# A new timetable for the last stage of a four-layer kernel: gating by half, four gate buffers, and a chain of small steps divided between VectorE and GpSimd

## The reference, cut to what matters

```python
def _L1_ffn_ref(x, Wm, bm, expert_emb, W1, b1, W2, b2, Wo, bo):
    BS, L, D = (4, 256, 128);  H, E, K = (8, 16, 2);  HD = D // H;  I = 512 // H
    h = x @ Wm + bm
    t = h.reshape(bs * L_ * H, HD)
    w = softmax(t @ expert_emb)                       # 16 weights for each head
    topw, topi = top_k(w, K)                          # ties: the lower index
    hmid = gelu(einsum('td,edi->tei', t, W1) + b1)    # 16 experts, 64 hidden each
    eo = einsum('tei,eio->teo', hmid, W2) + b2
    comb = (take_along_axis(eo, topi) * topw).sum(axis=1)
    return comb.reshape(bs, L_, d) @ Wo + bo
# x = x + _L1_ffn_ref(_layernorm(x), ...)
```

## Time and profile before

| | us |
|---|---|
| median of 3 runs | 2245.03 (2243.67 to 2245.81) |
| the profiled execution's own time | 2241.12 |
| its span | 2239.1 |
| head experts, first prologue matmul to the end | about 1770 to 2239 |
| of its stretch 1820 to 2239: PE busy / DVE / ACT / POOL | 399.3 / 300.1 / 284.1 / 86.5 of 419 |

### The profile page before, as it was taken

The page is one execution under the profiler, slowest core; times in us unless marked ns, Lnnn a source line. Parts: engine busy times, 40 slices in busy tenths (PEclk is TensorE's granted clock), DMA queues, the critical chain, the costliest instruction groups (busy, mean ns, idle before and its releaser), DMA issues. The chain is left out here.

```text
span 2239.1 us, 44674 instructions
## 1 busy us (share of the span) xinstructions
PE 1840.9 (82%) x16984; PEld 1141.9 (51%) x16984; DVE 1063.2 (47%) x2449; ACT 1334.1 (60%) x1479; POOL 214.8 (10%) x158
## 2 busy tenths in 40 slices
PE   3447999999994788787888878787887379999998
PEld 2337998989992443343443433343443145555554
DVE  6895222222225334433444334344441577777774
ACT  0013444444440597777778778677888156766675
POOL 7712000000003000000000000000000001211112
PEclk9567999999996799999999999899999589999999
DMA  6201000000002332133332222233220100000000
GB/s 220 52 14 41 1 1 1 1 2 1 1 1 56 69 74 58 41 73 74 71 73 59 68 56 51 64 73 71 58 58 5 56 1 6 6 5 5 5 5 10
DMA packets 37267, 88.90 MB, mean 40 GB/s; under 512 B 11481, under 2 KB 24034, under 8 KB 36466
## 3 DMA queue, kind: packets, MB, share of 16 engines
q1 hardware_dynamic: 33906, 78.82, 14.7%
q0 software_dynamic: 3072, 6.30, 1.4%
HBM read 33.15 MB, written 2.10 MB: 16 GB/s over the span
## 5 line engine op out<-in xcount | busy, mean ns | idle before, releaser
L1157 ACT ACTIVATE C_probs<-C_ps_s 128x1024 f32<-128x1024 f32 x832 | 781.9, 1070 | 243.5 <-PE C_ps_s L1084 241.3
L1097 PE MATMUL C_ps_o<-C_probs,C_values 128*16 128x256 f32 x6656 | 477.5, 401 | 30.1 <-DVE C_o_t L1270 16.1
L1592 ACT ACTIVATE D_hidden<-D_ps_u,D_b_up 128x1024 f32<-128x1024 f32 x256 | 275.3, 1113 | 150.0 <-PE D_ps_u L1508 149.9
L1084 PE MATMUL C_ps_s<-C_queries,C_keys 32*128 32x256 f32 x3328 | 222.2, 343 | 145.9 <-issue 59.5
L692 ACT ACTIVATE B_hidden<-B_ps_h,B_b_up 128x512 f32<-128x512 f32 x288 | 194.1, 687 | 187.8 <-PE B_ps_h L620 185.8
L1084 PEld LDWEIGHTS C_ps_s<-C_queries,C_keys 32*128 32x128 f32 x3328 | 133.8, 194 | 326.3 <-ACT C_probs L1157 174.7
L633 PE MATMUL B_ps_e<-B_w_down,B_hidden 128*128 128x128 f32 x2304 | 274.9, 276 | 0.0
L633 PEld LDWEIGHTS B_ps_e<-B_w_down,B_hidden 128*128 128x128 f32 x2304 | 269.9, 192 | 8.3
L1097 PEld LDWEIGHTS C_ps_o<-C_probs,C_values 128*16 128x16 f32 x6656 | 157.1, 98 | 193.9 <-issue 49.1
L1609 POOL TENSOR_TENSOR D_gated<-D_gated 128x1024 f32<-128x1024 f32 x32 | 76.2, 2382 | 1427.3 <-DVE D_gated L1725 1427.3
L787 DVE SCALAR_TENSOR_TENSOR B_acc<-B_ps_e,B_gate,B_acc 128x128 f32<-128x128 f32 x224 | 63.1, 344 | 289.2 <-PE B_ps_e L633 289.2
(11 more groups left out here) (259 smaller groups left out, 1967.9 us busy)
## 6 DMA issues: line engine op xcount, KB each, us to landing
C_keys<-C_k_hi SPq DMA_DIRECT2D x128, 200.1 KB, 4.3
C_ctx_t<-ctx_t_dram SPq DMA_DIRECT2D x16, 800.5 KB, 4.3
C_keys<-C_k_lo SPq DMA_DIRECT2D x64, 200.1 KB, 4.1
C_queries<-C_q_hi SPq DMA_DIRECT2D x128, 32.0 KB, 1.9
B_w_up<-L_ffn_w_up_dram SPq DMA_DIRECT2D x1, 2304.0 KB
B_w_down<-L_ffn_w_down_dram SPq DMA_DIRECT2D x1, 2304.0 KB, 20.8
A_ids<-ids_dram SPq DMA_DIRECT2D x1, 2048.0 KB
C_queries<-C_q_lo SPq DMA_DIRECT2D x64, 32.0 KB, 1.9
```

The lines of the kernel that those rows point to most:

```text
L1084: m = T.matmul(ps_s[bank(parity, 2 * step + j // 2)][:, j % 2, i, :], keys[rows, parity, g, kt * P:(kt + 1) * P], queries[rows, parity, g, ...
L1097: m = T.matmul(ps_o[32 * j:32 * j + 2 * DK, g % 2, :], values[:, parity, kt, g * HG + j, :], probs[:, slot(parity, 2 * step + j // 2), j % ...
L1157: nc.scalar.activation(probs[:, slot(parity, n)], ps_s[bank(parity, n)][:], ACT.Exp, scale=SCORE_SCALE1).then_inc(s_exp, 1)
L1592: nc.scalar.activation(hidden[:, u % RING, :, :], ps_u[u % 2][:], ACT.Gelu, bias=b_up[:, u % PAIRS:u % PAIRS + 1]).then_inc(s_hid, 1)
```

## The change

The tables are spread out: a job every even unit, a down piece every odd unit, and an out part every even unit from 14 on. Gating is done for each head (128x512) with a ring of four gate buffers. The exponential moves from unit 6 to unit 8, the first preparing job (turn) from 2 to 1, the turn_gate jobs from 26 and 30 to 29 and 31. Of the 16 steps of the choice, five go to GpSimd, and so do the two subtractions that make the low parts; each hand-over is a semaphore (`s_choice`). GpSimd's order within a block is written out in `body`.

```diff
+        PIECES = 2 * QUADS
+        GRING = 4
-        gate = sb("gate", [P, 2, 2, BLOCK])
+        gate = sb("gate", [P, GRING, BLOCK])
-        PREPARE = {2: ("turn", 0), 3: ("project", 0), 6: ("logit", 0), 7: ("place_up", 0), 10: ("place_up", 1),
-                   14: ("place_up", 2), 18: ("place_up", 3), 26: ("turn_gate", 0), 30: ("turn_gate", 1)}
+        PREPARE = {1: ("turn", 0), 3: ("project", 0), 5: ("logit", 0), 7: ("place_up", 0), 11: ("place_up", 1),
+                   15: ("place_up", 2), 25: ("place_up", 3), 29: ("turn_gate", 0), 31: ("turn_gate", 1)}
-        GATES = {4 * v + s: ("place_gate", (v, s)) for v in range(QUADS) for s in range(2)}
+        GATES = {2 * m: ("place_gate", m) for m in range(PIECES)}
-        EXP_AT, SPLIT_AT = 6, 25
+        EXP_AT = 8
-        CHOOSE_AT = {9: (0, 1, 2), 10: (3,), 13: (4,), 14: (5,), 17: (6, 7, 8), 18: (9,), 21: (10, 11, 12),
-                     22: (13,), 23: (14,), 24: (15,)}
+        CHOOSE_AT = {9: (0, 1), 11: (3,), 13: (4,), 17: (6, 7), 19: (8, 9), 21: (10,), 23: (12, 13)}
+        POOL_CHOICES = (2, 5, 11, 14, 15)
-        DOWN_AT = timetable((4 * v + 5 + s, (v, s)) for v in range(QUADS) for s in range(2))
-        GATING_AT = timetable((4 * v + 6, v) for v in range(QUADS))
-        OUT_AT = timetable((8 * hp + 15 + (0, 1, 4, 5)[n], (hp, n)) for hp in range(HP) for n in range(4))
+        DOWN_AT = timetable((2 * m + 5, (m,)) for m in range(PIECES))
+        GATING_AT = timetable((2 * m + 6, m) for m in range(PIECES))
+        OUT_AT = timetable((8 * hp + 14 + 2 * n, (hp, n)) for hp in range(HP) for n in range(4))
         X_AT = 13
         HEADS_AT = 4
+        SPLIT_AT = 27
...
+                def body(k, before, prepares):
+                    if before:
+                        add_groups(k - 1, HP - 1)
+                    if prepares:
+                        lower_heads(k + 1)
+                        choose(k + 1, 2)
+                    if before:
+                        add_bias(k - 1)
                     add_groups(k, 0)
-                    add_bias(k - 1)
-                    for hp in range(1, HP - 1):
-                        add_groups(k, hp)
+                    if prepares:
+                        choose(k + 1, 5)
+                    add_groups(k, 1)
+                    if prepares:
+                        choose(k + 1, 11)
+                        choose(k + 1, 14)
+                        choose(k + 1, 15)
+                    add_groups(k, 2)
+                    if prepares:
+                        lower_gates(k + 1)
...
-                    V.scalar_tensor_tensor(to, ps_e[:], b_down[:, v % EG:v % EG + 1], gate[:, v % 2],
+                    V.scalar_tensor_tensor(to, ps_e[:, s], b_down[:, v % EG:v % EG + 1], gate[:, piece % GRING],
                                            ALU.add, ALU.mult).then_inc(s_read, 1)
```

More of the change, by code:

```diff
@@ L1497, in job @@
                     else:
-                        v, s = arg
+                        v, s = divmod(arg, 2)
                         half, h = divmod(v // EG * 2 + s, HG1)
@@ L1510, in up, with down @@
                     m.then_inc(s_up, 1)
[L1512 to L1515, removed]
+                def down(k, piece):
+                    v, s = divmod(piece, 2)
+                    pe.wait_ge(s_hid, UNITS * k + 4 * v + 4)
+                    wait(pe, s_read, PIECES * k + piece - 1)
                     for i in range(4):
@@ L1566, in _ @@
                 pe.wait_ge(s_job_done, jobs_before(BLOCKS - 1) + NGATE)
-                for s in range(2):
-                    down(BLOCKS - 1, QUADS - 1, s)
+                for what, of_before in DOWN_AT.values():
+                    if of_before:
+                        down(BLOCKS - 1, *what)
                 for hp, n in (what for what, of_before in OUT_AT.values() if of_before):
@@ new lines, in choose @@
+                def choose(p, step):
+                    pool.wait_ge(s_choice, CHOICE_STEPS * p + step)
+                    if step == 2:
+                        ins = G.tensor_tensor(weight[:], weight[:], total[:].unsqueeze(2).to_broadcast(CHOICES),
+                                              ALU.mult)
+                    elif step == 14:
+                        ins = G.tensor_tensor(chosen[:, 0], chosen[:, 0], chosen[:, 1], ALU.add)
+                    elif step == 15:
+                        ins = G.tensor_tensor(weight[:], weight[:], chosen[:, 0], ALU.mult)
+                    else:
+                        ins = G.tensor_tensor(hit[:], hit[:], order[:].unsqueeze(1).to_broadcast(CHOICES), ALU.mult)
+                    ins.then_inc(s_choice, 1)
@@ L1654, in job @@
                     else:
-                        v, s = arg
-                        wait(dve, s_read, QUADS * p + v - 1)
-                        done = V.tensor_copy(gate[:, v % 2, s, :], ps_p[:])
+                        wait(dve, s_read, PIECES * p + arg - GRING + 1)
+                        done = V.tensor_copy(gate[:, arg % GRING, :], ps_p[:])
                     done.then_inc(s_job_done, 1)
@@ L1737, in experts @@
                     for u in range(UNITS):
+                        if u in GATING_AT:
+                            piece, of_before = GATING_AT[u]
+                            if not of_before:
+                                gating(k, piece)
+                            elif not first:
+                                gating(k - 1, piece)
                         if u in at:
@@ L1771, in _ @@
                         for step in range(CHOICE_STEPS):
-                            choose(0, step)
+                            if step not in POOL_CHOICES:
+                                choose(0, step)
                         split_gates(0, 0)
@@ L1784, in _ @@
                 rounds(dve, BLOCKS, experts)
-                gating(BLOCKS - 1, 1, QUADS - 1)
+                for piece, of_before in GATING_AT.values():
+                    if of_before:
+                        gating(BLOCKS - 1, piece)
                 add_to_stream(BLOCKS - 1)
```

78 lines of the change are left out of this document (38 added, 40 removed).

## The result

| | median, us | runs | against before |
|---|---|---|---|
| before | 2244.35 | 2242.51 to 2245.81 | |
| changed | 2332.16 | 2330.66 to 2334.06 | 1.0392 (95%: 1.0374 to 1.0410) |

What follows compares the result with a forecast made beforehand. TensorE's own pace was taken to bound the kernel. Steady blocks of 49.9 us work plus 12.3 waits, +8.6 six times, with first and last blocks, prologue and end summed to +61.7: median 2306 us, range 2278 to 2325.

Steps and rivals of the forecast that it cites:

- The quad: TensorE's four ups, two gates, two outs and two downs without preparing jobs: 5.64 us in the even timetable, 5.76 before.
- The jobs: A preparing block's nine extra TensorE jobs, priced by similar matmuls: 4.8 us per block.
- the gain of 3.7 a block: Per preparing block: 2.7 us of waiting won back and 1.0 us from the even timetable's shorter quads.
- unit 14, bias ahead of add: First head pair's out part waits for GpSimd's add behind add_bias: 3.5 us a block, 2.6 in the last.
- unit 29, low part behind add: turn_gate waits for the gates' low part, behind the third pair's add on GpSimd: 2.95 us a block.
- exponential: Up in unit 11 waits for ScalarE's chain with the exponential and two table loads: 2.3 us a block.
- turn: Turn job in unit 1 waits for VectorE's normalizations behind the copy of gate 0: 1.15 us a block.
- units 6, 7, 25: VectorE late after the cast of h and step 10 wait out GpSimd adds: 2.4 us of TensorE waiting per block.
- prologue: Without cover, five choice steps and the gates' low part on GpSimd lengthen the prologue: +4.1 us.
- Rival 1: Even timetable wins, all hand-overs hidden, first pair's add ending within 3.6 us of up 12's start: 2222 us; chance 0.06.
- Rival 2: Only GpSimd's order bites: waits in units 14 and 29 stay, others absorbed, gains come: 2266 us; chance 0.13.
- Rival 3: GpSimd is slower in the chain, including about 1 us for its loop turn, +2.4 per block: 2323 us; chance 0.13.

Runs made afterwards that it cites:

- filled_waits: Changed kernel with 12 spare TensorE matmuls ahead of each of two long waits (turn_gate in unit 29, first out part in unit 14); 1.0313 against before.
- both_orders: Changed kernel with, on GpSimd, the first pair's add ahead of the bias and the gates' low part ahead of the third pair's add; 1.0173 against before.
- the mended kernel: Changed kernel, GpSimd's orders mended, normalizations first in unit 0, exponential behind gelu 6, h rounded in unit 3, two steps moved, VectorE's loop written out; 1.0011.
- before_shared: Kernel before with only choice steps 2, 5, 11, 14 and 15 moved to GpSimd, old timetable and whole gatings; 1.0027 against before.
- before_bias_ahead: Kernel before with one edit: GpSimd's add_bias stands ahead of the first pair's add; 1.0087 against before.

## Why the prediction was wrong in its size

The mechanism of the waits was right, step by step, and the sum too small by 26 us (24 in the stage of the two traces). The step that failed is the sentence "TensorE's own work in a preparing block is 8 x 5.64 + 4.8 = 49.9 us", taken at full clock throughout. It failed twice.

*The clock.* I had seen 1.00 in the earlier trace rows and carried it into a kernel whose waits I had myself put at 3.5 and 2.95 us. Behind those TensorE ran at half clock. In the blocks 1 to 5 of the changed kernel (1877.65 to 2209.23) it is busy 277.8 us, 17.3 more than five times 52.1, with twelve stretches at half clock in them. That is 1.4 us for each, and by this price about 23 us for all sixteen, which is an estimate. filled_waits, which takes twelve of the sixteen away, gives back 1.0392 - 1.0313 = 0.0079, or 18 us.

*The pace.* At full clock a block's own work is 52.1 (both_orders), not 49.9. The quad was right: 5.60 against 5.64. The jobs weren't: priced at 4.8 by their kin, they cost 52.1 - 44.8 = 7.3. Between an up and a down, where a plain odd unit takes 1.64, the units with a job take 2.73 (project) and 2.76 (logit), so these cost 1.09 and 1.12 instead of 0.77 and 0.9. They are the smaller part of the miss. By the same distances in block 1 of both_orders, waits left out, the four place_up cost 0.72, 0.48, 0.74 and 0.73 (2.67, where 1.8 was booked), turn and the two turn_gates 0.65, 0.53 and 0.53 (1.7 for 1.3), and three times an even unit takes 1.40 to 1.43 instead of 1.16 where TensorE starts again behind a wait (0.75, booked nowhere). Timeline of PE of the changed kernel, starts:

```profile
1945.54 0.72 PE L1515 MATMUL D_ps_u<-D_up_in,D_w_up_r 128*128 128x512 f32 x2
1946.21 1.13 PE L1490 MATMUL D_ps_p<-D_xt,D_wm 128*128 128x512 f32 x2
1947.27 1.06 PE L1524 MATMUL D_ps_e<-D_hidden,D_w_down 128*32 128x512 f32 x8
1948.27 0.73 PE L1515 MATMUL D_ps_u<-D_up_in,D_w_up_r 128*128 128x512 f32 x2
```

The same error sat in the kernel before: "53.6 - 46.1 - 4.8 = 2.7 us of waiting" was 1.2 of waiting and 52.4 of work. So the gain of 3.7 a block (2.7 and 1.0) that I credited to the even timetable was never there: its own work is 0.3 us a block less (52.1 against 52.4), and what it could win back was 1.2, or 2.4 behind a loop turn. In the mended kernel it won none of it.

*The waits* were forecast at 12.3 a block. Measured are 10.0 between a short turn wait and the next, and 11.8 where the long one falls in:

| term | forecast | measured |
|---|---|---|
| unit 14, bias ahead of add | 3.5 (last block 2.6) | 2.95 (2.23) |
| unit 29, low part behind add | 2.95 | 2.82 |
| exponential | 2.3 | 2.18 (block 0: 2.99) |
| turn | 1.15 | 0.99, every second one 2.78 |
| units 6, 7, 25 | 2.4 | 0.55 (unit 6) + 0.55 (unit 25) |
| half gating | 0.72 | 0.745 |
| prologue | +4.1 | +3.5 |

Unit 14 came out shorter because add_to_stream ran 2.2 behind up 12 (1964.91) where I had 2.6. In units 6, 7 and 25 the lock came as forecast, with 1.93 for the cast and 2.29 for step 10, but less of it reached TensorE than I had booked. Two readings were wrong without weight in the sum: a hand-over to GpSimd takes 0.2 and not 0.05 to 0.1 (in the earlier trace rows add_to_stream ends at 1934.77 and the bias starts at 1934.98), and up didn't lose 0.4 to the exponential in the steady blocks before, where its rows show no idle time. The low work and the high waits nearly cancel: with its waits filled, a block takes 62.1 where 62.2 was forecast. What is left is the clock, by far the most of it, and the loop turn, which makes the turn's wait 1.8 us longer twice. Taking it out gives 1.0392 - 1.0339 = 0.0053 or 12 us by the ratios, whose intervals leave some 5 us either way, and 7.6 us in the stage of the two traces. For the loop turn I had the rows and took only one of them: the earlier trace rows are 53.58, and the next pair of turns was 54.82 apart; I took the quicker for all. In the old timetable, whose turn stood a unit later, only 1.2 to 1.4 of it reached TensorE.

*The rivals.* Rival 1 is refuted on both counts, its condition (the add in time) and its prize. Rival 2 named the two waits rightly, and mending both gives back 49 us; they were not alone. Rival 3 gives 2323, the nearest number of all, by a mechanism that isn't there: GpSimd's add takes 2.36, its bias 1.27, and no wait of TensorE shows a loop turn of GpSimd. That would have been luck.

Left open: why the same wait, of 2.8 us or of 2.2, is followed by half clock in one block and not in another; why VectorE's loop turn costs nothing in before_shared; and where the 2.8 us per block of before_bias_ahead go.

## What to carry to other kernels

Where a forecast contains a wait of a saturated TensorE near 3 us, book the half clock behind it too, here about 1.4 us for each, and count waits near 2 us as a risk of it; filling the wait with spare matmuls tests it in one run. Price a moved job by the distance between the starts on both sides of its place, in a unit that has it and one that hasn't, and not by the duration of its kin; and check a figure for "waiting" obtained by subtraction against the idle times in the brackets. Read more than one turn of a loop: an alternation between blocks is a term of its own. Here it grew from 1.2 to 1.8 us when the turn was moved a unit nearer to the loop turn.

## What the hardware showed that was not expected

- In the changed kernel TensorE's granted clock went from 1.00 to 0.50 behind each wait of 2.78 to 2.99 us, came back 3 to 3.5 us later, and stayed behind waits of 2.18 and 2.23. Over the traces of all runs but before_bias_ahead, in the blocks, it fell behind 87 of 93 waits of 2.7 to 3.2 us, 16 of 60 of 2.1 to 2.3, 5 of 16 of 1.6 to 1.8 and none of 62 of 1.0 to 1.3.
- Matmuls without use, put into the waits, made the kernel 0.8% faster.
- Writing a loop of three turns out for one engine took 0.2% off the kernel before, 0.5% off the changed one (0.3% by the traces). At the loop's turn VectorE issued nothing for 1.8 to 2.8 us in the traces of the kernels that have the loop, except in before_shared, where no such gap is.
- VectorE's cast of 128x512 took 1.93 us beside a GpSimd add that had begun 0.7 us earlier, and 0.43 alone. The difference of 1.5 is nearly what the add had still to run.
